# A two-layer image block on one NeuronCore: split recurrence steps, a new order across tiles, LN4's normalise on POOL, the last tile by image

## The reference, cut to what matters

```python
# layer 0: LN, w_in, 3x3 depthwise conv, four-way EMA mix, LN, w_out, residual; LN, MLP (exact gelu), residual
# layer 1, per position, C = 96, HID = 384, T = 8:
xn = _ln(x, norm1_scale, norm1_bias)                      # "LN3" in the kernel
u = xn @ Wu + bu
g = sigmoid(xn @ Wg + bg)
h = 0
for _ in range(8):
    h = g * (h @ A) + (1.0 - g) * u                       # the recurrence
x = x + h
xn2 = _ln(x, norm2_scale, norm2_bias)                     # "LN4"
m = gelu(xn2 @ mlp_w1 + mlp_b1)                           # tanh form
return x + (m @ mlp_w2 + mlp_b2)
```

## Time and profile before

| what | us |
|---|---|
| median of 3 runs | 244.82 |
| lowest, highest | 244.03, 245.47 |
| the profiled execution | 244.01 |
| its span from first to last instruction | 242.2 |
| PE busy | 231.8 (96%) |
| DVE busy | 186.7 (77%) |
| ACT busy | 132.9 (55%) |
| POOL busy | 128.4 (53%) |
| mean granted clock of PE | 0.99 |

### The profile page before, as it was taken

One profiled execution on the slowest core, in us unless ns is written; L12 is line 12 of the kernel. 1 busy time (PEld: TensorE's weight loads), 2 busy tenths in 40 slices (PEclk: granted clock), 3 DMA queues, 4 the chain that ended last, 5 costly groups with the idle time before them and its releaser, 6 DMA issues.

```text
span 242.2 us, 4138 instructions
## 1 busy us (share of the span) xinstructions
PE 231.8 (96%) x1384; PEld 187.2 (77%) x1384; DVE 186.7 (77%) x460; ACT 132.9 (55%) x300; POOL 128.4 (53%) x163
## 2 busy tenths in 40 slices
PE   8599898999999999999999999999999999999994
PEld 6488676969697979787787878778787878878674
DVE  5499999999999999995468596886858687685610
ACT  4547876768585866465824828172643727252341
POOL 6571977687859492927685443516153453314310
PEclk9979999999999999999999999999999999999998
DMA  6830000000000000000000000000101010010111
GB/s 127 280 113 3 1 1 1 3 0 0 3 0 1 3 1 0 3 0 0 0 3 1 0 3 0 3 31 4 32 1 32 3 32 0 3 32 0 37 32 32
DMA packets 5621, 4.99 MB, mean 21 GB/s; under 512 B 512, under 2 KB 5344, under 8 KB 5600
## 3 DMA queue, kind: packets, MB, share of 16 engines
q1 hardware_dynamic: 5168, 4.49, 5.9%
q10 hardware_dynamic: 432, 0.23, 0.7%
HBM read 3.15 MB, written 1.57 MB: 20 GB/s over the span
## 4 chain that ended last, share of the span: by engine, by line
PE 84%; DVE 9%; issue 3%; ACT 2%; POOL 1%; DVEq 0%; ACTq 0%; POOLq 0%
PE bank L1130 10%; PE pM L1086 8%; PE bank L1229 7%; PE pA L1130 7%; PE pM L1338 6%; PE bank L1064 6%; PE pM L1069 5%; PE pM L1070 4%; PE pM L1071 4%; PE bank L1264 3%; PE bank L1007 2%; PE bank L1019 2%; PE bank L1166 2%; PE bank L1269 2%; PE pA L1154 2%
## 5 line engine op out<-in xcount | busy, mean ns | idle before, releaser
L334 POOL TENSOR_TENSOR rs<-var,power 128x4 f32<-128x4 f32 x32 | 32.5, 1015 | 49.7 <-DVE var L764 49.6
L839 DVE SCALAR_TENSOR_TENSOR cA<-pA,cols,cA 128x528 f32<-128x528 f32 x56 | 42.4, 756 | 1.7 <-ACT cA L597 1.3
L911 DVE SCALAR_TENSOR_TENSOR q<-th,bank 96x256 f32<-96x256 f32 x48 | 19.9, 417 | 11.2 <-PE bank L1130 10.3
L839 DVE SCALAR_TENSOR_TENSOR cB<-bank,cols,cB 128x256 f32<-128x256 f32 x56 | 26.5, 473 | 0.0
L1338 PEld LDWEIGHTS pM<-w,hid 128*128 128x128 f32 x192 | 24.3, 192 | 1.2
L1130 PE MATMUL pA<-q,a_half 96*96 96x256 f32 x96 | 24.8, 380 | 0.1
L1338 PE MATMUL pM<-w,hid 128*128 128x96 f32 x192 | 24.3, 272 | 0.0
L1086 PE MATMUL pM<-w,hid 128*128 128x96 f32 x192 | 23.9, 272 | 0.0
L1086 PEld LDWEIGHTS pM<-w,hid 128*128 128x128 f32 x192 | 23.4, 192 | 0.5
L1229 PE MATMUL bank<-local,mix 128*128 128x384 f32 x64 | 22.1, 488 | 0.0
L331 POOL TENSOR_TENSOR xl<-xc,xh 96x512 fp32r<-96x512 f32 x15 | 19.0, 1269 | 5.3 <-ACT xh L494 5.2
(11 more groups left out here) (208 smaller groups left out, 576.7 us busy)
## 6 DMA issues: line engine op xcount, KB each, us to landing
x_all<-in_x SPq DMA_DIRECT2D x8, 192.0 KB, 2.7
out<-y SPq DMA_DIRECT2D x8, 192.0 KB, 2.0
w<-in_w SPq DMA_DIRECT2D x1, 480.0 KB, 7.4
w<-in_w SPq DMA_DIRECT2D x1, 336.0 KB, 6.6
mix<-in_mix SPq DMA_DIRECT2D x1, 256.0 KB, 6.8
w<-in_w SPq DMA_DIRECT2D x1, 144.0 KB, 3.1
rows<-in_rows ACTq DMA_DIRECT2D x1, 144.0 KB, 6.0
w<-in_w SPq DMA_DIRECT2D x1, 96.0 KB, 6.2
```

Of the source, the lines that this page charges most:

```text
L334: pool.tensor_tensor(rs[:, :], var[:, :], power[:, :], ALU.pow).then_inc(step, 1)
L839: dve.scalar_tensor_tensor(out=acc, in0=src, scalar=col(f"k{'AB'[grp]}{k}"), in1=acc, op0=ALU.mult, op1=ALU.add).then_inc(s["conv_step"], 1)
L911: dve.scalar_tensor_tensor(out=moved(c, k + 1)[0:D, half(h)], in0=th[c % 2][0:D, half(h)], scalar=1.0, in1=step_bank(k, h), op0=ALU.add, o ...
```

## The change

1. **Split steps.** For tiles 2 to 7, step 0 and steps 2 and 5 (tile 7: 0 and 2) are done in three fp32r passes, with a_h and a_l made once in `setup2`. The high parts are copies on ACT (`hs_split_high`, `q_split_high`), the low part of hs is made on POOL (`hs_split_low`), that of q on DVE (`q_split_low`).
2. **The next tile's g, u and hs within this pass.** g and u come in one piece after step 4 (tile 1: around step 4), evac_gu(f) on ACT after them, and first_h(f) on DVE after step 5. A pass of PE now begins with step 0, the MLP's products follow, and last_h of the tile before stands on DVE behind step 0.
3. **LN4's normalise** moves from ACT to POOL for tiles 0 to 6 (`normalize4`), ahead of add_q(c, 3).
4. **The last tile by image.** Its h8 transposes, x4, sums, xn4's transposes, splits, second MLP product, y and store are done in two halves, with banks of their own (M1_LAST, last_bank); ACT and DVE share the normalise. The matmuls of WARM_TAIL go.

hs has a semaphore of its own (hs_ready), so q_ready counts 14 to a tile and not 15.

```diff
-QS = 2 * STEPS - 1
+QS = 2 * (STEPS - 1)
 HALF_STEPS = 2 * (STEPS - 1)
-WARM_TAIL = (1, 3)
+M1_LAST = (2, 3, 1)
+SPLIT_LATER = (2, 5)
...
+        def split_step(c, k):
+            return 2 <= c < TILES and (k == 0 or (k in SPLIT_LATER and not (is_last(c) and k == SPLIT_LATER[1])))
...
+            def hs_split_low(c):
+                if split_step(c, 0):
+                    pool.wait_ge(s["hs_high"], c - 1)
+                    split_low(hs_l, hs[c % 2], hs_h).then_inc(s["hs_low"], 1)
+            def normalize4(m):
+                pool.wait_ge(s["x4_ready"], m + 1)
+                pool.wait_ge(s["ln4_step"], m + 1)
+                wait(pool, s["tr4_done"], m)
+                for k in range(CHUNKS):
+                    pool.tensor_scalar(xn4[:, k * D:(k + 1) * D], x4[:, k * D:(k + 1) * D], rs4[:, k:k + 1], None,
+                                       ALU.mult).then_inc(s["xn4_ready"], 1)
...
+                add_q(c, 1)
                 if tile_known(m):
                     pool.wait_ge(s["var4_ready"], m + 1)
                     wait(pool, s["xn4_ready"], 4 * m)
                     inverse_std(rs4, var4, s["ln4_step"])
-                add_q(c, 1)
+                    if not is_last(m):
+                        normalize4(m)
                 add_q(c, 3)
                 ln3_std(n)
+                hs_split_low(f)
...
+            def hs_split_high(c):
+                if split_step(c, 0):
+                    act.wait_ge(s["hs_ready"], c + 1)
+                    act.activation(hs_h[0:D, :], hs[c % 2][0:D, :], ACT.Copy).then_inc(s["hs_high"], 1)
+            def q_split_high(c, k):
+                if split_step(c, k):
+                    for h in range(2):
+                        act.wait_ge(s["q_ready"], QS * c + 2 * (k - 1) + h + 1)
+                        act.activation(qh[0:D, half(h)], moved(c, k)[0:D, half(h)], ACT.Copy)\
+                           .then_inc(s["qh_ready"], 1)
...
-                evac_gu(c)
+                normalize3(f)
                 gelu(0)
-                normalize3(f)
+                q_split_high(c, 2)
                 gelu(1)
                 gelu(2)
-                normalize4(m)
+                if is_last(m):
+                    normalize_last()
                 split3(f)
-                if tile_known(m):
+                q_split_high(c, 5)
+                evac_gu(f)
+                hs_split_high(f)
...
+            def q_split_low(c, k):
+                if split_step(c, k):
+                    for h in range(2):
+                        dve.wait_ge(s["qh_ready"], split_count(c, k, h))
+                        dve.tensor_tensor(ql[0:D, half(h)], moved(c, k)[0:D, half(h)], qh[0:D, half(h)].bitcast(F32),
+                                          ALU.subtract).then_inc(s["ql_ready"], 1)
...
+                if peeled(c, 1):
+                    add_h8(m)
+                    ln4_stats(m, between=lambda h: step(c, 0, [h]))
+                    step(c, 1)
+                    step(c, 2)
+                    step(c, 3)
+                elif tile_known(c):
                     step(c, 0)
-                step(c, 1)
-                step(c, 2)
-                step(c, 3)
+                    last_h(m)
+                    step(c, 1)
+                    add_h8(m)
+                    q_split_low(c, 2)
+                    step(c, 2)
+                    ln4_stats(m)
+                    step(c, 3)
+                elif is_last(m):
+                    last_h(m)
+                    ln4_last_stats(m)
+                ln3_low(f)
+                step(c, 4)
+                q_split_low(c, 5)
                 if tile_known(n):
                     ln3_stats(n)
-                ln3_low(f)
-                step(c, 4)
+                step(c, 5)
+                if tile_known(f):
+                    first_h(f)
+                ln4_low(m)
...
+                high, low = (hs_h, hs_l) if k == 0 else (qh, ql)
+                for h in range(2):
+                    res, first = step_bank(k, h), k not in (1, 3)
+                    if not split_step(c, k):
+                        if k == 0:
+                            pe.wait_ge(s["hs_ready"], c + 1)
+                        else:
+                            pe.wait_ge(s["q_ready"], QS * c + 2 * (k - 1) + h + 1)
+                        last = pe.matmul(res, a_half[0:D, :], moved(c, k)[0:D, half(h)],
+                                         start=first, stop=True, skip_group_check=True)
+                    else:
+                        if k == 0:
+                            pe.wait_ge(s["hs_high"], c - 1)
+                        else:
+                            pe.wait_ge(s["qh_ready"], split_count(c, k, h))
+                        pe.matmul(res, a_h[0:D, :], high[0:D, half(h)], start=first, stop=False,
+                                  skip_group_check=True)
+                        pe.matmul(res, a_l[0:D, :], high[0:D, half(h)], start=False, stop=False,
+                                  skip_group_check=True)
+                        if k == 0:
+                            pe.wait_ge(s["hs_low"], c - 1)
+                        else:
+                            pe.wait_ge(s["ql_ready"], split_count(c, k, h))
+                        last = pe.matmul(res, a_h[0:D, :], low[0:D, half(h)], start=False, stop=True,
+                                         skip_group_check=True)
+                    last.then_inc(s["step_done"], 1)
...
+                if peeled(c, 1):
+                    m1(0)
+                    h8_transposes()
+                    m1(1)
+                    rec_step(c, 0)
+                    m1(2)
+                    rec_step(c, 1)
                     ln3_transposes(f)
-                m2(0)
-                rec_step(c, 2)
-                m2(1)
-                rec_step(c, 3)
-                if is_last(m):
-                    keep_warm(WARM_TAIL[0])
+                    m2(0)
+                    rec_step(c, 2)
+                    m2(1)
+                    rec_step(c, 3)
+                    gu_next(0)
+                    rec_step(c, 4)
+                    gu_next(1)
                     ln4_transposes(m)
-                m2(2)
-                rec_step(c, 4)
-                if tile_known(m) and not is_last(m):
+                    rec_step(c, 5)
+                    m2(2)
+                    rec_step(c, 6)
...
+                elif tile_known(c):
+                    rec_step(c, 0)
+                    m1(0)
+                    rec_step(c, 1)
+                    h8_transposes()
+                    m1(1)
+                    m1(2)
+                    rec_step(c, 2)
+                    ln3_transposes(f)
+                    rec_step(c, 3)
+                    m2(0)
+                    rec_step(c, 4)
+                    gu_next(0)
+                    gu_next(1)
+                    rec_step(c, 5)
+                    ln4_transposes(m)
+                    m2(1)
+                    m2(2)
+                    rec_step(c, 6)
...
+                def gu_next(k):
+                    if not tile_known(f):
+                        return
+                    if peeled(c, 1):
+                        pe.wait_ge(s["gelu_done"], 3 * (TILES - 1) + 2 + k)
+                    else:
+                        pe.wait_ge(s["gelu1_done"], 3 * g + 2 + k)
+                    gu(f, k)
...
+            def ln4_last_stats(m):
+                wait(dve, s["xn4_ready"], 4 * m)
+                wait(dve, s["x4b_ready"], m)
+                wait(dve, s["ln4_step"], m)
+                for h in range(2):
+                    dve.wait_ge(s["trh_done"], m + 1 + h)
+                    dve.tensor_tensor(x4[:, chunks(h)], last_bank(h)[:, 0:2 * D], x_tile(m)[:, chunks(h)], ALU.add)\
+                       .then_inc(s["x4_ready"], 1)
+                    dve.wait_ge(s["x4_ready"], m + 1 + h)
+                    dve.bn_stats(st4[:, 6 * h:6 * h + 6], pairs(x4)[h]).then_inc(s["bn4_step"], 1)
+                dve.wait_ge(s["bn4_step"], 2 * m + 2)
+                dve.tensor_scalar(var4[:, :], st4[:, 2:12:3], 1.0 / D, EPS1, ALU.mult, ALU.add)\
+                   .then_inc(s["var4_ready"], 1)
+                ln4_last(m)
...
-            for t in range(TILES):
+            for t in range(TILES - 1):
                 sp.wait_ge(s["y_ready"], t + 1)
                 sp.dma_start(out_d[t], y[:, :].rearrange("p (i f) -> p i f", i=2)).then_inc(s["y_stored"], 16)
-            sp.wait_ge(s["y_stored"], 16 * TILES)
+            for h in range(2):
+                sp.wait_ge(s["y_ready"], TILES + h)
+                sp.dma_start(out_d[TILES - 1][:, h, :], y[:, chunks(h)]).then_inc(s["y_stored"], 16)
+            sp.wait_ge(s["y_stored"], 16 * (TILES + 1))
```

220 lines of the change are left out of this document (150 added, 70 removed).

## The result

The changed kernel takes **254.1 us** (254.05 to 254.31) where the kernel before, on the same chip, takes 244.5 (244.03 to 245.47): a ratio of **1.039, 95% interval 1.035 to 1.042**. The forecast was 243.4 with a range to 249.8; it was wrong, in its sign too. The profiled execution lasts 254.06 us, its span is 252.27 us.

What follows compares the result with a forecast made beforehand. PE was taken to bound the kernel (84% of the chain of waits). Middle passes -1.5, tile 1 +2.6 and the end -2.4 sum to -1.3 to -1.4 us; off 244.82 that gives 243.4 us, range 240.4 to 249.8.

Steps and rivals of the forecast that it cites:

- The port: Rival: POOL's add_q(c,1) gets in between h's halves, 1.05 us in six tiles, 249.7 us; chance 0.24 including two hits.
- The sum for the middle passes: Five middle passes fall from 68.4 to 66.9 us, a gain of 1.5, at 13.4 us a pass.
- rows 10: Trace rows near 117 us where DVE's th-nu operation (0.81 us) and POOL's rsm (1.46) each look held by the other.
- The second hit: Port rival's further case: step 5's low part on DVE held by add_q(c,3), which starts within 0.1 us of it.
- LN3's sums: DVE's work for LN3 in a middle pass, after step 5's low parts, taken at 0.73 us.
- both: Rival with port hits on h and on step 5's low part: near 255 us, chance 0.07.
- PE's own pace: Middle pass on PE alone: 13.4 us of work before, 12.9 with three split steps, each 0.155 us cheaper.
- The old wait of 0.38 us behind xl3: PE's one wait in a middle pass before, xn4's transposes behind DVE's xl3; it was to go.
- The border of step 0: Between tiles, the round DVE - ScalarE - DVE paces: stalls of 0.35 us for hs_l and 0.15 before step 1.
- Tile 1: Tile 1's pass slower by 2.6 us, from a 1.4 us stall ahead of g and a late hs_l; bounds 1.2 to 3.
- The end: Last tile and draining passes from 28.5 to 26.1 us, -2.4, with a new 0.8 us stall for xn4; bounds -1.5 to -3.3.
- Setup: Ahead of 131.49 us: a_h and a_l made once at body0(3), each under 0.45 us, taken as costing nothing.

Runs made afterwards that it cites:

- e1: Changed kernel plus one wait: POOL starts adding step 1's q to hs only after DVE has finished both halves of h; 248.2 us.
- e2: Changed kernel with POOL's LN3 inverse standard deviation moved ahead of its addition of step 3's q; 251.1 us (one execution).
- e5: Changed kernel with e1's wait and, in all tiles but tile 1, e2's order on POOL; 246.0 us, ratio 1.010.
- e9: Changed kernel with h made by DVE in one operation of 512 columns, not two of 256; 248.4 us.
- e8: e6 with no step split, all seven in full fp32; 242.0 us, ratio 0.994.
- e10: e8 with steps 2 and 5 split again into three fp32r passes, step 0 left in fp32; 241.55 us, ratio 0.988.
- e6: e5 with xl3 made on DVE ahead of step 3's q in tile 1; 243.9 us, ratio 1.000.

## Why the prediction was wrong, step by step

- **The port: the step that failed.** The sum for the middle passes (66.9 us) left both halves of h at 0.41 us and LN3's variance inside 0.73 us of sums, that is, it put waiting for POOL at nothing. The mechanism, its place (the second half of h) and its price (1.05 us, six times) stood among the rivals, with a chance of 0.24. Measured: the half is 1.08 us longer, six times, and e1 takes 5.9 us back. What failed is the argument against it, that in rows 10 "it was DVE, waiting, that got in ahead of POOL's next". That row shows the side that waits getting in at the next border between two instructions; here it was POOL that waited, and the border lay between DVE's halves. Read so, the row spoke for the hit.
- **The second hit** was put on step 5's low part. That was nearly untouched (0.89 us for its two halves in tile 2, 0.74 bare); the addition started later, since POOL's four LN4 operations lasted 2.0 to 2.3 us and not 1.7, and fell on LN3's variance, which I had priced within "LN3's sums" and never held against POOL's row. The earlier trace rows show just this: a four-column variance held under a two-input operation of POOL. It cost 0.82 us a pass (e2). The time for "both" was given as near 255, with a chance of 0.07, and left out of the range. That the result lies so near is in part luck, as the second hit fell at another operation than the one named.
- **The port is not all of it.** With both hits gone (e5) the time is 246.0, 2.6 above the forecast. Between the same marks (start of tile 1's pass, first product with hs_l of tile 2, of tile 7, end) e5 has 16.3, 68.0 and 27.0 us; forecast were 16.3, 66.9 and 26.1. The next points say where the 1.1 and the 0.9 lie.
- **The Trainium skill**, "SBUF — State Buffer", section "Who interferes with whom", has the rule (a DVE instruction with two SBUF inputs contends with a GpSimd one that reads SBUF; whoever issues first has the pair for the whole instruction). The trace agrees at h, 1.49 us under POOL's addition, and e9 the other way round, POOL's 1.67 under DVE's h. It does not at POOL's inverse root: the first h, two inputs, lasts its bare 0.68 us at 161.16 inside one (from 160.67, 1.04 us). For the additions the rule held, and its time, 249.7 or more, was the better forecast.
- **PE's own pace: right.** 13.4 us unsplit was forecast, 13.41 measured (e8); 0.155 us a split step, 0.15 measured (e10 against e8). The old wait of 0.38 us behind xl3 is gone.
- **The border of step 0: right in kind, too small.** The forecast had 0.35 us of waiting for hs_l and 0.15 ahead of q_one. Measured from start to start with the port free (e6): 0.60 for hs_l, 0.07 behind it, and no wait ahead of q_one. PE's pace with three split steps was right: 13.41 less three times 0.155 is 12.95 (forecast 12.9), and with 0.67 the measured 13.62 instead of 13.4; 1.1 us in five passes. (PE counts as busy for 13.19 of 13.62, as busy time includes 0.16 us of a record's drain ahead of the wait.) So the split of step 0, booked as a gain of 0.155, costs 0.67 - 0.155 = 0.52 (e6 against e10).
- **Tile 1: right.** +2.6 forecast, +2.5 measured. PE is idle for 1.20 us ahead of g, released by xl3 (forecast 1.4), and hs_l's product of tile 2 starts at 148.65; forecast was 147.8 or, with the 0.83 by which this execution was late, 148.63.
- **The end: right in its parts, not in its sum.** From the last h's transposes on it is 12.9 us (239.34 to 252.27) for 15.5 before (226.71 to 242.19). Against the 26.1 forecast, 28.25: the sixth hit on h 1.05, PE idle 1.21 instead of 0.8 ahead of xn4 (POOL's four operations 2.02 us and not 1.7), and 0.45 between step 6 and the end of the three products, where h stands beside POOL's x4b. Of the other 0.24, 0.15 is the mark, which lies ahead of hs_l's product; 0.1 I can't place.
- **Setup: nothing**, as taken. The +0.8 ahead of 132.32 is the spread of executions: in the fifteen profiled executions, which differ there in no more than a_h and a_l, tile 0's step 0 starts between 120.0 and 122.0 us, the first of them in e9, which has both.
- **What would have shown it:** the text asked whether h lasts 0.41 us or over 1 us. It was the line that decided.
